# Two large attentions: separate waits for rows of queries and of keys, queries fetched two steps sooner, projections taken one maximum later, 32 columns of V

## The reference, cut to what matters

```python
# A: 16 heads of 8; window of 128 keys, own position excluded; mixed by a gate with a latent attention
q, k, v = jnp.split(x @ qkv_w + qkv_b, 3, axis=-1)
scores = jnp.where(allowed, einsum('bhqd,bhkd->bhqk', q, k) / sqrt(8), NEG)
local = softmax(scores) @ v
gate = sigmoid(local @ gl_w + remote_h @ gr_w)
out = (gate * local + (1 - gate) * remote_h) @ out_w + out_b
# B: 16 heads of 8, causal over 256 keys, rotary positions on q and k
out = softmax(causal(rope(x @ Wq) @ rope(x @ Wk).T / sqrt(8))) @ (x @ Wv) @ Wo
```

## Time and profile before

| | us |
|---|---|
| median of 3 runs | 6852.19 |
| profiled execution, its own time | 6882.46 |
| its span (first to last instruction) | 6880.6 |
| TensorE (PE) busy | 5494.3 (80%) |
| VectorE (DVE) busy | 4304.2 (63%) |
| ScalarE (ACT) busy | 2877.9 (42%) |
| GpSimd (POOL) busy | 3251.0 (47%) |
| loop of the 64 steps, stage `loc` | 3732 to 4518 |
| loop of the 64 steps, stage `cau` | 5408 to 6124 |

### The profile page before, as it was taken

One profiled execution on the slowest core, in us unless ns is written; L12 is line 12 of the kernel. 1 busy time (PEld: TensorE's weight loads), 2 busy tenths in 40 slices (PEclk: granted clock), 3 DMA queues, 4 the chain that ended last, 5 costly groups with the idle time before them and its releaser, 6 DMA issues. The chain is left out here.

```text
span 6880.6 us, 81795 instructions
## 1 busy us (share of the span) xinstructions
PE 5494.3 (80%) x22762; PEld 2782.0 (40%) x22762; DVE 4304.2 (63%) x6292; ACT 2877.9 (42%) x4905; POOL 3251.0 (47%) x2381
## 2 busy tenths in 40 slices
PE   5888888888868887788896888965797688885797
PEld 1333333333324435342584444423564234433465
DVE  5999999999984730565323666753575455553575
ACT  4656666566644532344321444431232244441232
POOL 2888888788863510243211333325433344434433
...
DMA packets 174785, 476.04 MB, mean 69 GB/s; under 512 B 29648, under 2 KB 54992, under 8 KB 146640
## 3 DMA queue, kind: packets, MB, share of 16 engines
...
## 5 line engine op out<-in xcount | busy, mean ns | idle before, releaser
L337 POOL TENSOR_TENSOR mamba_bu<-mamba_du,mamba_b_all 128x1024 f32<-128x1024 f32 x512 | 1200.9, 2356 | 280.9 <-DVE mamba_hc L599 269.3
L592 DVE TENSOR_TENSOR_SCAN mamba_bu<-psum,mamba_bu 128x512 f32<-128x512 f32 x1024 | 1192.6, 1205 | 157.2 <-ACT psum L529 124.2
L428 PE MATMUL psum<-mamba_hc,consts 128*128 128x512 f32 x2048 | 1014.7, 620 | 20.5 <-DVE mamba_du L604 20.5
L529 ACT ACTIVATE psum<-mamba_delta,A 128x510 f32<-128x510 f32 x1024 | 684.6, 685 | 572.8 <-DVE mamba_bu L592 558.6
L599 DVE TENSOR_TENSOR mamba_hc<-mamba_bu,psum 128x1024 f32<-128x1024 f32 x512 | 611.2, 1194 | 6.0 <-PE psum L419 6.0
L428 PEld LDWEIGHTS psum<-mamba_hc,consts 128*128 128x128 f32 x2048 | 402.9, 198 | 368.9 <-issue 349.6
L1598 POOL DMA_INDIRECT results<-ffn_moe_y_rows,ffn_moe_row_of x312 | 302.0, 968 | 508.8 <-DVE ffn_moe_y_rows L1788 433.2
L2363 POOL TENSOR_TENSOR loc_q_bd<-loc_q_max,weights_l1a 128x512 fp32r<-128x512 f32 x256 | 274.9, 1102 | 543.6 <-DVE loc_q_max L2597 526.1
L1713 ACT ACTIVATE ffn_moe_act<-ffn_moe_act 128x512 f32<-128x512 f32 x344 | 216.9, 631 | 722.8 <-DVE ffn_moe_act L1757 722.7
L2427 PE MATMUL psum<-consts 128*128 128x256 bf16 (+1 forms) x1024 | 284.9, 320 | 235.6 <-issue 175.5
L419 PE MATMUL psum<-mamba_parts,consts 128*128 128x512 bf16 x512 | 201.7, 394 | 334.4 <-DVE mamba_hc L599 332.4
...
## 6 DMA issues: line engine op xcount, KB each, us to landing
mamba_b_all<-b_rows SPq DMA_DIRECT2D x128, 1024.0 KB, 6.3
...
```

The source lines that it names most:

```text
L337: nc.gpsimd.tensor_tensor(bu[:, J % BU, :, :], du[:, q % 2, :, :], b, ALU.mult).then_inc(bu_ready, 1)
L428: nc.tensor.matmul(ysum[h], mem.ident, hc[:, J % HC, h, :], start=(n == 0), stop=(n == NST - 1), skip_group_check=True).then_inc(summed, 1)
L529: nc.scalar.activation(by_seq(dA[i % DECAYS])[:, :, 1:S], by_seq(delta[:, q % 2, h, :])[:, :, 1:S], ACT.Exp, scale=mem.A[:, q % 2, h * NST ...
L592: nc.vector.tensor_tensor_scan(bu[:, J % BU, h, :], dA[i % DECAYS], bu[:, J % BU, h, :], 0.0, ALU.mult, ALU.add).then_inc(scanned, 1)
```

## The change

Five edits, all in `stacked_attention`:

1. `st_landed` becomes `q_landed` and `k_landed`. The first scores of a tile wait for the queries' 12 transfers, the first turned scores (two steps later) for the keys' 12.
2. `spread_rows` becomes `spread_queries` and `spread_keys`. Queries of tile t+1 are sent at the end of the loop turn of tile t, when `add_max` of step 4t-1 has released the buffer; ahead of the loop they go before the first `k_bd`.
3. `store_rows(t+1)` stands behind the keys of tile t in both stages (in `cau` it stood behind `spread_diagonal(2t+1)`), and it also waits for the landing of the keys that used its slot.
4. VectorE takes a projection behind the first maximum of the next part (`take_work`), and behind `add_max` where that part opens a step.
5. A weigh's product takes 32 columns of V instead of 9, so `v` is laid out flat with 23 columns more, and all of it is set to 1.0 at the start (2004 elements a partition instead of 192). The rows of PSUM that the added columns write are not used.

The diff:

```diff
--- before.py
+++ after.py
@@ -2164,6 +2164,7 @@
 G, GH = 4, 4
 PARTS = 3
 MAX_ROW = 24
+WIDE = 32
 STEPS_A = NSEQ * QB
 T_LAG, O_LAG = 2, 3
 
@@ -2183,7 +2184,7 @@
         qk = sb("qk", 2, 2, T, dt=F32R)
         turned = sb("rope", 2, 2, T) if rope else None
         whole = sb("whole", 2, T) if rope else None
-        v = sb("v", VR, SUB, HEADS, HD + 1)
+        v = sb("v", VR, SUB, HEADS * (HD + 1) + WIDE - HD - 1)
         q_st = sb("q_st", 2, G, T, dt=F32R)
         k_st = sb("k_st", 2, G, T, dt=F32R)
         k_bd = sb("k_bd", 2, G, GH, S, dt=F32R)
@@ -2197,7 +2198,8 @@
          t_ready, powers_ready, weighed, sums_ready, tok_ready, inverted, masked, heads_ready) = ctx.enter_context(signals(
              nc, stage, "work", "work_read", "hi", "lo", "turned", "whole", "v_stored", "zeroed", "rows_stored", "s", "s_read", "q_max", "q_bd", "t", "powers",
              "weighed", "sums", "tok", "inverted", "masked", "heads"))
-        st_landed = ctx.enter_context(signals(nc, stage + "_st_landed", *"01"))
+        q_landed = ctx.enter_context(signals(nc, stage + "_q_landed", *"01"))
+        k_landed = ctx.enter_context(signals(nc, stage + "_k_landed", *"01"))
         bd_landed = ctx.enter_context(signals(nc, stage + "_bd_landed", *"01"))
         if mix is not None:
             mix.allocate(nc, ctx, stage)
@@ -2290,15 +2292,22 @@
                 sp.dma_start(dram[tile % 2].rearrange("a p t -> p a t"), qk[:, :, :, :].bitcast(F32).rearrange("p a b t -> p (a b) t")).then_inc(rows_stored, 16)
                 sp.wait_ge(rows_stored, 16 * (tile + 1) + LEAD)
 
-            def spread_rows(tile):
+            def spread(name, to, tile, landed):
+                for i in range(GH):
+                    for part in range(PARTS):
+                        rows = dram[tile % 2, source(name, part), 32 * i:32 * i + 32, :].rearrange("(g j) t -> j g t", g=G)
+                        at = 32 * i + HD * part
+                        sp.dma_start(to[at:at + HD, tile % 2, :, :].bitcast(F32), rows).then_inc(landed[tile % 2], 16)
+
+            def spread_queries(tile):
+                if tile >= 2:
+                    sp.wait_ge(q_max_ready, 4 * (tile - 1) + LEAD)
+                spread("q", q_st, tile, q_landed)
+
+            def spread_keys(tile):
                 if tile >= 2:
                     sp.wait_ge(t_ready, t_count[4 * (tile - 1)] + LEAD)
-                for name, to in (("q", q_st), ("k", k_st)):
-                    for i in range(GH):
-                        for part in range(PARTS):
-                            rows = dram[tile % 2, source(name, part), 32 * i:32 * i + 32, :].rearrange("(g j) t -> j g t", g=G)
-                            at = 32 * i + HD * part
-                            sp.dma_start(to[at:at + HD, tile % 2, :, :].bitcast(F32), rows).then_inc(st_landed[tile % 2], 16)
+                spread("k", k_st, tile, k_landed)
 
             def spread_diagonal(b):
                 if b >= 2:
@@ -2317,28 +2326,30 @@
 
             store_rows(0)
             sp.wait_ge(zeroed, 6 + LEAD)
+            spread_queries(0)
             spread_diagonal(0)
-            spread_rows(0)
+            spread_keys(0)
             spread_diagonal(1)
             load_latents(0)
             store_rows(1)
+            spread_queries(1)
             for tile in range(1, NT):
                 spread_diagonal(2 * tile)
-                spread_rows(tile)
-                if rope:
-                    spread_diagonal(2 * tile + 1)
+                spread_keys(tile)
                 if tile + 1 < NT:
+                    sp.wait_ge(k_landed[(tile - 1) % 2], 16 * 12 * ((tile - 1) // 2 + 1) + LEAD)
                     sp.wait_ge(bd_landed[1], 16 * 12 * tile + LEAD)
                     store_rows(tile + 1)
-                if not rope:
-                    spread_diagonal(2 * tile + 1)
+                spread_diagonal(2 * tile + 1)
                 load_latents(tile)
+                if tile + 1 < NT:
+                    spread_queries(tile + 1)
 
         @block.gpsimd
         def _(pool):
             nc.gpsimd.memset(q_st[:, :, :, :].bitcast(F32), 0.0).then_inc(zeroed, 1)
             nc.gpsimd.memset(top[:, :, :], 0.0).then_inc(zeroed, 1)
-            nc.gpsimd.memset(v[:, :, :, :, HD:HD + 1], 1.0).then_inc(zeroed, 1)
+            nc.gpsimd.memset(v[:, :, :], 1.0).then_inc(zeroed, 1)
 
             def add_rope(a, tile):
                 pool.wait_ge(turned_ready, 4 * tile + 2 * a + 2 + LEAD)
@@ -2420,7 +2431,7 @@
                 keys = (qb + 1) * 128
                 if k == 0:
                     pe.wait_ge(bd_landed[b % 2], 16 * 12 * (b // 2 + 1) + LEAD)
-                    pe.wait_ge(st_landed[tile % 2], 16 * 24 * (tile // 2 + 1) + LEAD)
+                    pe.wait_ge(q_landed[tile % 2], 16 * 12 * (tile // 2 + 1) + LEAD)
                 pe.wait_ge(s_read, number - 1 + LEAD)
                 to = mem.bank[S_BANK[number % 2]].rearrange("p (h k) -> p h k", h=n)
                 for m, (c, mask) in enumerate(masks[qb]):
@@ -2441,6 +2452,7 @@
                 g, c = t_units(s)[k]
                 number = t_number(s, k)
                 if k == 0:
+                    pe.wait_ge(k_landed[tile % 2], 16 * 12 * (tile // 2 + 1) + LEAD)
                     pe.wait_ge(q_bd_ready, s + 1 + LEAD)
                 pe.wait_ge(powers_ready, number - 1 + LEAD)
                 to = mem.bank[T_BANK[number % 2]].rearrange("p (h q) -> p h q", h=GH)
@@ -2461,8 +2473,9 @@
                     pe.wait_ge(v_stored, tile + 1 + LEAD)
                 pe.wait_ge(powers_ready, number + 1 + LEAD)
                 for i in range(GH):
-                    last = nc.tensor.matmul(mem.psum[32 * i:32 * i + HD + 1, O_BANK[s % 2], g * 128:(g + 1) * 128],
-                                            v[:, tile % VR, in_b * QB + c, GH * i + g, :], powers[:, number % PT, i * 128:(i + 1) * 128],
+                    at = (GH * i + g) * (HD + 1)
+                    last = nc.tensor.matmul(mem.psum[32 * i:32 * i + WIDE, O_BANK[s % 2], g * 128:(g + 1) * 128],
+                                            v[:, tile % VR, in_b * QB + c, at:at + WIDE], powers[:, number % PT, i * 128:(i + 1) * 128],
                                             start=(c == 0), stop=(c == qb), skip_group_check=True)
                 last.then_inc(weighed, 1)
 
@@ -2569,7 +2582,7 @@
                 dve.wait_ge(work_ready, taken(("v", tile)) + LEAD)
                 if tile >= VR:
                     dve.wait_ge(weighed, t_count[4 * (tile - VR + 1)] + LEAD)
-                to = v[:, tile % VR, :, :, 0:HD]
+                to = v[:, tile % VR, :, 0:HEADS * (HD + 1)].rearrange("p a (h e) -> p a h e", h=HEADS)[:, :, :, 0:HD]
                 for j in range(SUB):
                     src = work[:, j * D:(j + 1) * D].rearrange("p (h d) -> p h d", h=HEADS)
                     if rope:
@@ -2615,6 +2628,16 @@
                     dve.wait_ge(work_ready, taken(("out", s - 2)) + LEAD)
                 done = heads_ready if mix is None else mix.local_ready
                 nc.vector.tensor_tensor(out, total[:, :, :, 0:HD], by_head, ALU.mult).then_inc(done, 1)
+
+            def take_work(s, part):
+                for name, i in work_uses(s, part):
+                    if name in inputs:
+                        if rope:
+                            turn(inputs.index(name), i)
+                        else:
+                            low(name, i)
+                    if name == "v":
+                        take_v(i)
 
             nc.vector.memset(k_bd[:, :, :, :, :].bitcast(F32), 0.0).then_inc(zeroed, 1)
             if mix is not None:
@@ -2635,14 +2658,8 @@
                             maximum(s, k)
                         if k == 0 and 1 <= s <= STEPS_A:
                             add_max(s - 1)
-                    for name, i in work_uses(s, part):
-                        if name in inputs:
-                            if rope:
-                                turn(inputs.index(name), i)
-                            else:
-                                low(name, i)
-                        if name == "v":
-                            take_v(i)
+                        if k == ks[0] and (s or part):
+                            take_work(*((s, part - 1) if part else (s - 1, 3)))
                     if part == 3 and 0 <= s - O_LAG < STEPS_A:
                         finish(s - O_LAG)
                     if mix is not None and 0 <= s - O_LAG - 1 < STEPS_A:
```

## The result

The changed kernel takes **6654.76 us** (median of 4 runs, 6644.32 to 6657.88) against 6860.52 for the kernel before (4 runs, three of them those of the table above): ratio 0.9707, interval 0.9677 to 0.9737, 206 us less. A second comparison, all runs on one chip, gave 0.9676 (0.962 to 0.9732), 225 us less. The forecast was 6600 with a range of 6560 to 6705: the direction, the mechanism and the range hold, the middle lies 55 us too low. The profiled execution takes 6655.68 us (span 6653.6) against 6882.46, 227 us less.

The account below looks back on a forecast made before the run. TensorE, the busiest engine, loses time to late transfers at tile starts, VectorE waits and a lowered clock. Gains of 122 (`loc`), 120 (`cau`) and 18 (starts) less 8 (loads) make 252 us off 6852.19: 6600 us, range 6560 to 6705.

Parts of the forecast that it names:

- Tile starts: Both loops: keys off the path to first scores and queries sooner give every tile the time without late transfers.
- the undisturbed one: Tile without late transfers, at full clock: 42.45 us in `loc`, 38.70 in `cau`; with edit 4, forecast 41.4 and 37.2.
- Start: Ahead of each stage's first scores: the keys' 0.79 MB go behind, 9 us a stage, 18 us in all.
- Late next: `loc` tiles after edit 4: `work` becomes late, so VectorE's wait of 2.12 us becomes 1.05.
- Edit 5: 768 weighs: 23 more columns add 10 ns a load, counted as 10 ns a weigh, 8 us lost.
- A (DMA engines): DMA engines become the bound; 2 us of wait plus 1.5 of clock return in 31 tiles: 6710 us, chance 0.12.
- B: VectorE or bank `work` becomes the bound; 2 us a tile in `loc`, 1 in `cau`: 6645 us, chance 0.15.
- C: A weigh's eight wider loads no longer overlap in the added columns, 61 us instead of 8: 6653 us, chance 0.06.
- D: A weigh's products stop running side by side, 0.64 us more a weigh, 492 us: 7092 us, chance 0.02.
- E: The wait only moves from the keys to the second `k_bd` behind a later store: about 6804 us, chance 0.03.
- What would show it: Signs: no L2427 wait over 1.5 us in loops, clock above 0.98, loops about 665 and 598 us, `q_st` issued last.
- The fear at the end: Both stages: if shorter waits still cost the full clock, about 3 us a tile stay, 90 us.

Follow-up runs that it names:

- old takes: Changed kernel, but VectorE takes projections where it did before, behind the part's own maxima and ahead of `finish`; 32 columns kept: 6684.72 us, ratio 0.9774.
- edit 1 alone: Kernel before with only separate waits for queries and keys, order of transfers unchanged: 6719.24 us, ratio 0.9815.
- edit 4 alone: Kernel before with only VectorE's takes of projections moved behind the next maximum: 6818.92 us, ratio 0.9918.
- late queries: Changed kernel, but a tile's queries are fetched behind its own first `k_bd` again, ahead of the keys; separate waits kept: 6660.7 us, ratio 0.9751.

## Why the prediction was right, and where it was off

**Tile starts: right.** The forecast gave every tile the time of the undisturbed one, 41.4 us in `loc` and 37.2 in `cau`. A tile is now 41.14 and 37.64 on the mean. The forecast's own sum lay 0.25 a tile higher with the loads, so the tiles came out 0.5 us shorter and 0.2 longer. Reading the clock's share off a tile that has no late rows, and not adding waits and clock apart, is what made this hold. How the gain splits between the edits was less right: edits 1 to 3 were to give `loc` the tile of 42.45 us. With the old takes it is 44.53, of which 0.3 are the loads, because the clock falls behind most waits of 2.1 us. So edit 4 was worth 3.4 us a tile in `loc`, not 1.05; the sum held because both were made together.

**Attentions as a whole: right.** 252 us forecast, 247 found between the two profiles: `loc` 121.7 against 131 (122 and 9 for the start), `cau` 125.3 against 129, with the loads inside. Between the means of three profiles each (1594.3 and 1358.4) it is 236. Its parts by the stages: edit 1 alone 177, edit 4 alone 42, edit 4 on top of the others 60, queries two steps sooner on top of the others 35. They do not add up, since each depends on what the others have left.

**Start: right in `cau`, mis-sized in `loc`.** The first scores come 12.9 us sooner after the stage's start in `cau` and 11.5 in `loc`, for 9 each; between the means of three profiles it is 11.0 and 7.5. But `loc` gives back its share in the 10.4 us and the lower clock after it (0.61 in 3722 to 3735): its first tile takes 43.6 us on the mean where kernels without this wait need 33 to 36. The step that failed is the 9 us for `loc` in the term of 18. It counted how much sooner the first scores come and not what else the steps behind them need. The queries of the second tile were covered, as the prediction says ("steps 0 to 3, some 35 us, cover them"), and for what stands behind the store only TensorE waits. But the store itself has a waiter, ScalarE's `high`, and behind it the copy of the sums. I had followed what is queued behind SyncE's wait, and not who needs the waiting transfer itself. In `loc` late queries showed what it can cost: 30 us.

**Late next: pessimistic.** I left 1.05 us a tile in `loc` for `work`. The rows show 2.0 us for `loc_both` and 2.0 for maxima in the whole loop. This is why the forecast of 10 to 16 us of waits for maxima was too high. That the sum for `loc` comes so near (122 for 131) is partly luck: these 8 us or so made up for much of what the start gave back.

**Edit 5: near, by a wrong load.** Some 11 us by the tiles in place of 8. The load is 19 ns longer, not the 10 of the line through 9 and 128 columns, and a weigh is longer by one load's 19, of which the tiles show 12 to 15. The line went through the wrong row: other loads of 128 columns of the same type take longer than the 140 to 143 ns of L2436, in the same loop of before

```profile
L2451 PEld LDWEIGHTS psum<-loc_q_bd,loc_k_st x384: 190/201/358, 3749.5 to 4515.3; 128*128 128x128 f32 x192
```

and a line to their 201 ns gives an estimated 22 ns for 23 columns. The larger clearing of `v` takes 1.77 us on GpSimd where the prediction estimated 1.3; it ends at 3684.5, ahead of the first store (3693.45), and is hidden.

The Trainium skill ("TensorE: Matmul & The Clock Gate", LDWEIGHTS) gives columns over 1.2 ns; by that 23 columns are an estimated 19 ns. The trace agrees with this difference, at 86/89 and 105/108 ns, but not with the durations, which by the page would be an estimated 7.5 and 27 ns. The 118 us that the prediction reckoned for eight such loads in a row did not come.

**The middle of the range.** From 6600 to 6654.8 are 55 us. 30 of them are a step of method: the sum was worked out from a profiled execution 30 us above the median and then taken whole off the median. The excess seems to lie partly in what the change removes; that is a pattern over 13 profiles, and no run isolates it. The profiled executions of kernels that still wait at tile starts lie 22, 21, 17 and 38 us above the median of their runs (before three times, the first against 6860.52; edit 4 alone); those of the nine others with a median beside them lie between 14 below and 16 above. Against its own profile the forecast was 6630. Another 26 are the feed-forwards, which go with the batch, 5 the sum, and 6 go the other way, ahead of `loc`.

**Rivals.** A (DMA engines) did not come: their share rose from 0.31 to 0.38 in `cau` without a wait. B did not: past the start no waits for `work` over 2.0 us in all. C did not: the eight loads still overlap, and of eight times 19 ns one comes. D is out, a weigh takes 0.36 us. E is out, no wait at a second `k_bd`. Of the signs under "What would show it", four held (no wait at a tile's start, the clock, the order of the queue, the weigh). The loops are 680 and 604 us for 665 and 598: in `loc` mostly by the wait of 10.4 us, which stands before a projection and not before a score unit, and its clock. The waits at the stages' starts (8.3 and 8.0 us for 12) and for maxima (2.0 us in `loc` for 10 to 16, 3.1 in `cau` for under 8) are lower than forecast. The fear at the end, that shorter waits still cost the clock, is true of waits of 2.1 us in `loc`, as the old takes showed; in the changed kernel no such waits are left.
